# State products of 102 columns in two PSUM banks, their three parts added on VectorE and GpSimd, and two exchanges in the order

## What is computed

```python
x = x + attn(layernorm(x), w_qkv, w_out)
x = x + ffn(layernorm(x), Wg, Wu, Wd, Wr, temperature)
# attn: q, k = elu(rope(q) * s) + 1, elu(rope(k) * s) + 1; then over tokens, per head:
kv = kv + k_t v_t^T ; ks = ks + k_t
out_t = (q_t kv) / max(q_t . ks, 1e-6)
# ffn: weights w[t, e] by a router with a fallback to the best two experts
out = sum_e w[:, e] * ((silu(x Wg_e) * (x Wu_e)) Wd_e)
```

## Time and profile before

| | us |
|---|---|
| median of 3 runs | 798.66 (795.63 to 800.37) |
| the profiled execution | 795.7 |
| its span | 793.7 |
| TensorE busy (share) | 770.3 (97%) |
| VectorE busy | 606.7 (76%) |
| ScalarE busy | 465.6 (59%) |
| GpSimd busy | 483.3 (61%) |
| granted TensorE clock | 0.993 |

### The profile page before, as it was taken

One profiled execution on the slowest core, in us unless ns is written; L12 is line 12 of the kernel. 1 busy time (PEld: TensorE's weight loads), 2 busy tenths in 40 slices (PEclk: granted clock), 3 DMA queues, 4 the chain that ended last, 5 costly groups with the idle time before them and its releaser, 6 DMA issues.

```text
span 793.7 us, 18504 instructions
## 1 busy us (share of the span) xinstructions
PE 770.3 (97%) x6882; PEld 667.3 (84%) x6882; DVE 606.7 (76%) x1597; ACT 465.6 (59%) x886; POOL 483.3 (61%) x537
## 2 busy tenths in 40 slices
PE   8877899999999999999999999999999999999998
PEld 8766688888888888888888888888888888888887
DVE  6798888878777797779877797778887788756344
ACT  3665767666666656666666566656656665644222
POOL 3795778755566576655666665565676656653322
PEclk9999999999999999999999999999999999999999
DMA  4555214122111121222101221120311121100000
GB/s 143 129 120 98 69 54 93 41 44 69 41 41 23 22 67 41 42 43 58 39 15 40 43 68 41 41 43 14 56 42 41 41 55 28 28 2 28 1 1 27
DMA packets 97321, 38.30 MB, mean 48 GB/s; under 512 B 74192, under 2 KB 96976, under 8 KB 97232
## 3 DMA queue, kind: packets, MB, share of 16 engines
q1 hardware_dynamic: 90704, 30.83, 18.2%
q10 hardware_dynamic: 6528, 6.29, 2.7%
HBM read 16.13 MB, written 4.19 MB: 26 GB/s over the span
## 4 chain that ended last, share of the span: by engine, by line
PE 85%; DVE 6%; POOL 2%; DMA 2%; issue 2%; ACT 2%; SPq 1%; DVEq 0%; ACTq 0%; POOLq 0%
PE y L486 22%; PE gate L452 21%; PE up L452 21%; PE front L312 5%; PE back L364 3%; PE back L408 3%; PE front L313 2%; PE up L383 2%; PE up L420 1%; POOL a_lo L1199 1%; PE front L335 1%; PE back L352 1%; PE back L395 1%; PE front L433 1%; PE back L335 1%
## 5 line engine op out<-in xcount | busy, mean ns | idle before, releaser
L1228 POOL TENSOR_TENSOR h_lo<-work,h_hi 128x512 fp32r<-128x512 f32 x126 | 163.2, 1295 | 59.2 <-ACT h_hi L688 59.2
L1199 POOL TENSOR_TENSOR a_lo<-am,a_hi 128x512 f16<-128x512 f32 x120 | 145.0, 1210 | 53.9 <-ACT a_hi L615 51.4
L486 PE MATMUL y<-wd_hi,h_hi 128*128 128x256 f32 x504 | 145.8, 289 | 0.0
L486 PE MATMUL y<-wd_lo,h_hi 128*128 128x256 f32 x504 | 140.4, 279 | 0.0
L486 PE MATMUL y<-wd_hi,h_lo 128*128 128x256 f32 x504 | 140.2, 278 | 0.0
L1072 DVE TENSOR_TENSOR work<-work,up 128x512 f32<-128x512 f32 x128 | 87.0, 679 | 61.7 <-PE up L452 61.4
L688 ACT ACTIVATE h_hi<-work 128x512 fp32r<-128x512 f32 x126 | 79.4, 630 | 58.2 <-DVE work L1072 36.4
L1088 DVE SCALAR_TENSOR_TENSOR xa<-y,wo,xa 128x256 f32<-128x256 f32 x252 | 111.9, 470 | 1.9 <-PE y L486 1.9
L486 PEld LDWEIGHTS y<-wd_hi,h_hi 128*128 128x128 f32 x504 | 94.7, 188 | 4.1
L486 PEld LDWEIGHTS y<-wd_lo,h_hi 128*128 128x128 f32 x504 | 94.9, 188 | 2.8
L615 ACT ACTIVATE a_hi<-am 128x512 f16<-128x512 f32 x120 | 74.8, 624 | 35.4 <-DVE am L850 35.4
(11 more groups left out here) (228 smaller groups left out, 1774.3 us busy)
## 6 DMA issues: line engine op xcount, KB each, us to landing
xr<-xT SPq DMA_DIRECT2D x32, 128.0 KB, 2.4
xa<-x SPq DMA_DIRECT2D x32, 128.0 KB, 2.6
out<-xa SPq DMA_DIRECT2D x32, 128.0 KB, 1.7
xa<-Wg ACTq DMA_DIRECT2D x8, 256.0 KB, 2.8
work<-Wd ACTq DMA_DIRECT2D x8, 256.0 KB, 3.1
work<-Wu ACTq DMA_DIRECT2D x8, 256.0 KB, 2.9
work<-w_qkv SPq DMA_DIRECT2D x2, 384.0 KB, 3.8
qT<-q_st SPq DMA_TRANSPOSE x32, 3.2
```

What stands on the lines that cost most here:

```text
L486: m = pe.matmul(y_bank(n, t), h_at(hi, n)[:, t * P:(t + 1) * P], wd_p[wi][:, u // KI, u % KI, :], start=(n % KI == 0 and (t % 2 == 0 or n ...
L1199: pool.tensor_tensor(a_p[1][:, heads(r), :], am_place(g, r).rearrange("p (h n) -> p h n", h=4), a_p[0][:, heads(r), :], ALU.subtract).then ...
L1228: pool.tensor_tensor(h_at(1, n), hb[:, n % 2, :], h_at(0, n).bitcast(F32), ALU.subtract).then_inc(s_hlo, 1)
```

## The change

From tile 8 on (PARTS = 8), one product per pair of heads multiplies k by all three parts of v at once: 102 columns, 8 products. The three parts lie side by side and are added later. As 8 x 102 columns do not fit a bank, pairs 0 to 4 go to U in `state(c)`, pairs 5 to 7 to R1 in `av(c)`, between its products with a_hi and a_lo and those with the old state. VectorE keeps three running sums (`st_p`, in the space of the `stage` buffer, free by then): `st_add` adds U's five pairs (255 elements on half of the partitions, twice), the new `st_add_r1` R1's three pairs (153, twice). `st_parts` starts them, once, in the step of tile 7. GpSimd's new `st_sum` adds the three sums into `st_s`, in two instructions, and `s1` waits for it. `scores` waits for st_add_r1, since they write R1. On VectorE, st_add_r1 stands between norm and route_second, and o_lo goes ahead of k_lo. On ScalarE v_copy goes ahead of fb.

```diff
+            def state_parts(g, bank, first, last, done):
+                if bank is R1:
+                    w.wait_ge(s_v, tiles(g + 1))
+                for p in range(first, last):
+                    m = pe.matmul(bank[:, (p - first) * 2 * WV:(p - first + 1) * 2 * WV],
+                                  k_st[:, g % 2, 2 * p:2 * p + 2, :, :].rearrange("p h c d -> p (h c d)"),
+                                  vx[:, g % 2, 2 * p:2 * p + 2, :, :].rearrange("p h s d -> p (h s d)"),
+                                  start=(p == first), stop=(p == last - 1), skip_group_check=True)
+                m.then_inc(done, 1)
...
+                if g >= PARTS:
+                    state_parts(g, R1, NPU, NP, s_stater)
                 if g >= NT:
                     from_state(False, True)
...
+                if g >= PARTS:
+                    state_parts(g, U, 0, NPU, s_state)
+                    return
                 for p in range(NP):
                     for j in range(3):
...
+                if g > PARTS:
+                    w.wait_ge(s_ssr, 2 * (g - PARTS))
...
+            def parts_add(bank, first, last, done):
+                new = bank[:, 0:(last - first) * 2 * WV].rearrange("p (q h s d) -> p q h s d", q=last - first, h=2, s=3)
+                for hh in range(2):
+                    rows = slice(64 * hh, 64 * hh + 64)
+                    v.scalar_tensor_tensor(out=st_p[rows, first:last, :, :], in0=new[rows, :, hh, :, :], scalar=ASCALE,
+                                           in1=st_p[rows, first:last, :, :], op0=ALU.mult, op1=ALU.add).then_inc(done, 1)
...
+                if g >= PARTS:
+                    w.wait_ge(s_stp, 2)
+                    w.wait_ge(s_sum, g - PARTS)
+                    parts_add(U, 0, NPU, s_ss)
+                    return
...
+            def st_sum(g):
+                w.wait_ge(s_ss, 2 * g + 2)
+                w.wait_ge(s_ssr, 2 * (g - PARTS) + 2)
+                w.wait_ge(s_s1, g)
+                w.wait_ge(s_sr, g)
+                pool.tensor_tensor(st_s[:, :, :], st_p[:, :, 0, :], st_p[:, :, 1, :], ALU.add).then_inc(s_sum1, 1)
+                w.wait_ge(s_sum1, g - PARTS + 1)
+                pool.tensor_tensor(st_s[:, :, :], st_s[:, :, :], st_p[:, :, 2, :], ALU.add).then_inc(s_sum, 1)
...
-                th(router); qk_copy(a); slab_hi(slab(s, 1)); fb(router); v_copy(a); e1(router); exp(a); silu(n + 1)
+                th(router); qk_copy(a); slab_hi(slab(s, 1)); v_copy(a); fb(router); e1(router); exp(a); silu(n + 1)
...
-                route_first(router); norm(c); route_second(router); q_lo(a); k_lo(a); o_lo(c); h_up(n + 1)
+                route_first(router); norm(c); st_add_r1(c); route_second(router); st_parts(c); q_lo(a); o_lo(c); k_lo(a); h_up(n + 1)
...
-                slab_lo(slab(s, 1)); v_rest(a); h_lo(n); h_lo(n + 1); slab_lo(slab(s, 2)); rstd2_pow(c); st_rest(c)
+                slab_lo(slab(s, 1)); st_sum(c); v_rest(a); h_lo(n); h_lo(n + 1); slab_lo(slab(s, 2)); rstd2_pow(c); st_rest(c)
```

More of the change, by code:

```diff
@@ L45 @@
 LAST = UNITS * NB - 4
+PARTS = 8
+NPU = 5
 def bcast(ap, axis, n):
@@ L145, in build @@
         hb, stage = work[:, 0:2, :], work[:, 2:4, :]
+        st_p = stage[:, 0, 0:NP * WV].rearrange("p (q s d) -> p q s d", q=NP, s=3)
         h_p = [sb(f"h_{s}", [P, 2, B], F32R) for s in ("hi", "lo")]
@@ L171, in build @@
              "slab_hi", "slab_lo"))
-        (s_qkv, s_qk, s_av, s_state, s_oT, s_proj, s_x2T, s_lgrows, s_logit, s_gate, s_up, s_down, s_last) = (
+        (s_qkv, s_qk, s_av, s_state, s_oT, s_proj, s_x2T, s_lgrows, s_logit, s_gate, s_up, s_down, s_last, s_stater) = (
             sem(n) for n in ("qkv", "scores", "av", "state", "o_T", "proj", "x2_T", "logit_rows", "logit", "gate", "up",
-                             "down", "down_last"))
+                             "down", "down_last", "state_r1"))
         (s_xhi, s_qkc, s_v, s_exp, s_qhi, s_khi, s_v1, s_v2, s_ahi, s_s1, s_s2, s_ohi, s_lgc, s_th, s_e1, s_fb,
@@ L182, in build @@
         (s_slab_lov, s_xlo, s_bn, s_mv, s_ve, s_tcos, s_cos, s_rope, s_phi, s_qlo, s_klo, s_amask, s_o, s_ss, s_den, s_rec, s_norm, s_olo, s_x1,
-         s_bn2, s_mv2, s_ve2, s_x2n, s_x2lo, s_h, s_acc, s_hlov) = (sem(n) for n in (
+         s_bn2, s_mv2, s_ve2, s_x2n, s_x2lo, s_h, s_acc, s_hlov, s_stp, s_ssr) = (sem(n) for n in (
              "slab_lo_v", "x_lo", "bn", "mv", "ve", "tcos", "cos", "rope", "phi", "q_lo", "k_lo", "masked", "o", "ss", "den", "rec", "norm",
-             "o_lo", "x1", "bn2", "mv2", "ve2", "x2n", "x2_lo", "h", "acc", "h_lo_v"))
+             "o_lo", "x1", "bn2", "mv2", "ve2", "x2n", "x2_lo", "h", "acc", "h_lo_v", "state_parts", "ss_r1"))
         ROUTE = ("sum", "inh", "off", "zone", "dist", "zone2", "m", "eq", "w0", "c", "ws", "ix", "no", "s1", "nd",
@@ L188, in build @@
         s_route = sem("router_step")
-        s_rstd1, s_sin, s_vr, s_v3, s_alo, s_sr, s_s3, s_rstd2, s_hlo = (sem(n) for n in (
-            "rstd1", "sin", "vr", "v3", "a_lo", "sr", "s3", "rstd2", "h_lo"))
+        s_rstd1, s_sin, s_vr, s_v3, s_alo, s_sr, s_s3, s_rstd2, s_hlo, s_sum1, s_sum = (sem(n) for n in (
+            "rstd1", "sin", "vr", "v3", "a_lo", "sr", "s3", "rstd2", "h_lo", "st_sum1", "st_sum"))
         def routed(b, step):
@@ L623, in s1 @@
                 w.wait_ge(s_ss, 2 * g + 2)
+                if g >= PARTS:
+                    w.wait_ge(s_sum, g - PARTS + 1)
                 act.activation(st_x[:, :, 0, :], st_s[:, :, :], ACT.Copy).then_inc(s_s1, 1)
@@ L883, in st_add, with st_parts, st_add_r1 @@
                                            op0=ALU.mult, op1=ALU.add).then_inc(s_ss, 1)
+            def st_parts(g):
+                if g != PARTS - 1:
+                    return
+                for n in range(SLABS - NSL, SLABS):
+                    w.wait_ge(*slab_lo_done(n))
+                w.wait_ge(s_ss, 2 * PARTS)
+                v.memset(st_p[:, :, 1:3, :], 0.0).then_inc(s_stp, 1)
+                v.tensor_copy(st_p[:, :, 0, :], st_s[:, :, :]).then_inc(s_stp, 1)
+            def st_add_r1(g):
+                if not live(g) or g < PARTS:
+                    return
+                w.wait_ge(s_stp, 2)
+                w.wait_ge(s_sum, g - PARTS)
+                w.wait_ge(s_stater, g - PARTS + 1)
+                parts_add(R1, NPU, NP, s_ssr)
             def den_max(g):
```

## The result

The changed kernel takes 807.53 us (median of six executions) against 796.07 for the kernel before, both measured side by side. One of the six ran in a slower state, 1065.62 us at a granted clock of 0.655, so that the comparison rests on the other five, whose median is 806.21 us. Their ratio to the kernel before is 1.013, with a 95% interval from 1.0106 to 1.0153. The change makes the kernel slower by about 10 us; the forecast had 4.3. The profiled execution has a span 9.7 us longer than before.

What follows compares the result with a forecast made beforehand. TensorE was taken to bound the kernel, with VectorE's chain within a tenth of a microsecond; 23 steps x 0.20 = +4.6 us, less 0.26 in tile 31, gives +4.3 on 798.66: 803.0 us, range 797.0 to 808.0.

Steps and rivals of the forecast that it cites:

- Direction and mechanism: Slower: h_up(n+1), queued behind o_lo and k_lo on VectorE, makes TensorE's up(n+2) start 0.20 us later per step.
- One sign: In the list of waits, TensorE's proj would no longer wait for VectorE's o_lo; before, 27 waits, 7.0 us in all.
- Products: On TensorE, eight 102-column products at 0.045 us replace 24 small ones taking 0.62 us: 0.26 us less per tile.
- The additions of 255 elements: In VectorE's st_add, each addition takes 0.42 us plus a 0.03 gap, the pair 0.90 to 0.91.
- B: Rival: st_add's additions overlap what follows by 0.08 us instead of a 0.03 gap; not slower, 797.9 us; chance 0.08.
- C: Rival: additions at 0.47 us and products at 0.07 cost 0.10 per step each, router steps spill; 808.8 us; chance 0.15.
- C's third part: With the dearer additions and products, router steps would spill too, by 0.2 us in six steps.
- the head of the chain: From the state products through st_add to rope: rope 0.13 us earlier, less 0.01 for one more semaphore, so 0.12.
- costs nothing, with nothing to spare: In router steps VectorE's q_lo starts 0.32 us later, but VectorE is free for o_lo level with o_hi's release.
- an idle stretch: GpSimd's two added additions, 0.44 us each, run in 3.90 us of idle time ahead of v_rest.
- tile 31: The last tile's step, with no next tile on VectorE, would gain 0.26 us.
- Rival A: TensorE's saving arrives: 0.34 us per step in 23 steps, 0.26 in the last; 8.1 us faster, 790.6; chance 0.13.

Runs made afterwards that it cites:

- e2: The kernel before, with VectorE's o_lo ahead of k_lo and nothing else changed; ratio 1.0085 to the kernel before.
- e3: The changed kernel with VectorE's k_lo moved behind h_up(n+1), o_lo still first; ratio 0.9981 to the kernel before.
- e10: The changed kernel with two waits (s_s1, s_sr) no longer made ahead of st_add from tile 8 on; one execution, 804.1 us.
- e4: The changed kernel with GpSimd's st_sum behind v_rest instead of ahead of it; ratio 1.0261 to the kernel before.
- e6: The changed kernel with k_lo behind h_up(n+1) and route_second ahead of st_add_r1 on VectorE; ratio 1.0067 to the kernel before.
- e9: e6 plus GpSimd's st_sum behind h_lo(n+1) in router steps, and st_add without the waits for s_s1 and s_sr from tile 8; ratio 0.9934.

## Why the prediction was right, and where it was short

**Direction and mechanism: right.** TensorE's saving arrived and bought nothing; h_up(n+1) took o_lo's place as what holds TensorE, and up(n+2) waits for it, 23 times and 9.7 / 23 = 0.42 us each. e2 shows it without the split, e3 takes it away. One sign failed: the wait for o_lo did not go, it stands in the list 24 times with 8.4 us. The time, 807.5 (806.2 as the median of the five), is inside the range (797 to 808), near its edge, since the forecast's +4.3 us was less than half of what came. That it is inside at all is in part luck. The forecast stood on 798.66 us, and the kernel before took 796.07 side by side; on that base the forecast is 800.4 and the range 794.4 to 805.4, and both values lie above it.

**Products.** 0.045 us each was forecast, the trace has (0.41 - 0.21) / 4 = 0.05 at most; five took 0.24 for 0.23. The additions of 255 elements took (0.88 - 0.03) / 2 = 0.42 us each, as computed, and the gap of 0.03 held. So B fell, and of C the dear additions and products. C's third part, router steps that spill, came, and larger than C had it, and the time lies nearer to C's 808.8 than to the forecast's 803.0. The Trainium skill's 81 ns for a matmul of 128 columns in a stream of weight loads ("TensorE: Matmul & The Clock Gate", "Back-to-back issue gap") is not what these products show either.

**First mis-sized term: the head of the chain.** I took 0.01 us for one more semaphore ahead of st_add. The profile has rope 0.05 us earlier than before, not 0.12, and a step 0.27 longer, not 0.20. e10 shows how the term should have been worked out: not what one more wait adds, but that waits which stand in instructions of their own cost 0.15 to 0.21 us between the products and st_add, and a wait carried by st_add itself 0.03. Over 17 steps the miss is 1.2 us.

**Second: router steps, "costs nothing, with nothing to spare".** I had q_lo 6.30 us into the step; it came at 6.79. Of these 0.49 us, 0.39 is that route_second's instructions were held by GpSimd's additions, which I had put into "an idle stretch" of GpSimd without asking what VectorE does in it. e4 and e6 remove it (q_lo at 6.40 and 6.28). It cost six steps 0.5 us more than forecast, 2.9 us.

**Third, an omission.** The exchange sits in the steady loop and so also in the steps of tiles 4 to 7, where nothing else changes. The profile has 0.37 to 0.39 us per step there, 1.5 us; I counted 23 steps where it is 27. The three add up to 5.6 us; with the 0.26 of tile 31 and the 4.3 forecast that is 10.2, for the 10.1 measured from tile 4 on.

**Tile 31** was said to gain 0.26 us. From tile 31 to the end both kernels take 89.5 us, so nothing of it shows. In its step the five products took 0.36 us, not 0.24, and up(n+2) started only 0.06 us earlier than before (8.32 for 8.38). Why, and where the 0.06 went, was not tried.

**Rival A** (TensorE's saving arrives) needed o_hi released earlier, I wrote. It needed less: k_lo out of the way of h_up. With that, e3 gains 0.49 us an ordinary step over the change. Over the kernel before it gains only 0.21 of A's 0.34, and its router steps are 0.36 longer.

## What to carry to other kernels

When a step is moved ahead on an engine that runs in order, look first at whether its own input is there: if it has to wait, all behind it waits too, and the one to check is whoever releases the bottleneck engine (here h_up for up), not the step that was moved. A saving on the bottleneck engine counts only up to the next wait in its list, so compute both arrival times, its own and that of the signal. And additions put into idle time of GpSimd are not free by that alone: check who is queued behind them there, and which two-operand instructions of VectorE run at that moment.

## What the runs showed of the hardware

VectorE instructions that read two operands from SBUF were held where a GpSimd instruction was already running, and ended about 0.05 us behind it: 32 elements took 0.36 and 0.40 us beside additions of 136 elements, and 0.66 to 1.22 beside h_lo (1.3 us), for 0.18 to 0.19 alone. One that had started first kept its time (L1068, 0.19 us, with GpSimd's addition starting 0.10 us into it). k_lo and h_up, which read one operand from SBUF and one from PSUM, keep 0.68 us beside the same h_lo. The Trainium skill says it in "SBUF — State Buffer", "Who interferes with whom": a VectorE instruction with two SBUF inputs contends with a GpSimd instruction that reads SBUF, and one with at most one such input doesn't, as long as it runs in none of the modes that use both ports. By that rule the trace agrees in all these cases. One instruction was held that has a single input, in every router step of both kernels: L1114 of the changed kernel (4 elements) took 0.61 us and ended with GpSimd's a_lo; a like one, L1062, took 0.16 with nothing beside it.

The distance between a signal and its instruction depends on how the wait is written: 0.03 us where st_add carries the wait for the products itself (e10), 0.15 with the wait for the products in an instruction of its own (before), 0.21 with that and a second one behind it (changed). In the changed kernel, where this chain sets the pace, that was worth 0.18 us a step (e10), more than the 0.14 of the split in e3; in e9, where it mostly does not, 0.02 to 0.10 us an ordinary step.
